# Four graph layers at the edges' nodes: destinations ended in the last aggregation, messages for the source side alone, a head projection of its own

## The reference

```python
# layer 2: attention with 8 heads, self loops included
h = (x @ W_src).reshape(n, 8, 16)
e = leaky_relu(a_src[src] + a_dst[dst])
alpha = softmax of e over the edges of one dst
out = segment_sum(h[src] * alpha, dst) + bias
# layer 3: here `dst` of the layer is the edge's source
h = features @ W_neigh.T + b_neigh
new_h = concat([h[src], abs(h[dst] - h[src])]) @ W_edge.T + b_edge
seg_sum = segment_sum(new_h, dst); cnt = segment_sum(1, dst)
s = (h + seg_sum) / max(cnt, 1)
z = concat([features, s]) @ W_lin.T + b_lin
```

## Time and profile before

| | us |
|---|---|
| median of 3 runs (3661.37 to 3671.05) | 3662.82 |
| profiled execution | 3684.87 |
| its span, first to last instruction | 3683.2 |
| POOL busy | 2036.5 |
| PE busy | 2249.8 |
| DVE busy | 2173.2 |
| ACT busy | 1669.2 |
| mean granted TensorE clock | 0.794 |

### The profile page before, as it was taken

How to read it: one execution, slowest core, us unless ns; L and a number is a source line. 1 busy time by engine, 2 the same in 40 slices (tenths; PEclk the granted TensorE clock), 3 DMA queues, 4 the chain that set the end, 5 groups by cost and what they waited for, 6 DMA issues and landing times. The chain is left out here.

```text
span 3683.2 us, 52863 instructions
## 1 busy us (share of the span) xinstructions
PE 2249.8 (61%) x12839; PEld 1786.9 (49%) x12839; DVE 2173.2 (59%) x7930; ACT 1669.2 (45%) x3697; POOL 2036.5 (55%) x2221
## 2 busy tenths in 40 slices
PE   2316899998999675446556655874553644545442
PEld 1303666766677564446445553553543533333332
DVE  5516998998999686433534636944558533443242
ACT  0016999999998485222322335832441122222100
POOL 3878765665573431468038336703550058888767
PEclk9998999999999877567757757985666667777665
DMA  2511132332331262754266284425330534343363
GB/s 80 170 41 30 44 98 85 101 99 86 99 98 41 81 181 75 195 131 122 60 183 175 60 229 109 116 82 145 93 79 15 160 90 98 85 99 84 58 184 93
DMA packets 592914, 382.51 MB, mean 104 GB/s; under 512 B 50669, under 2 KB 540622, under 8 KB 592266
## 3 DMA queue, kind: packets, MB, share of 16 engines
q1 hardware_dynamic: 537050, 338.44, 31.5%
q0 software_dynamic: 52800, 39.73, 6.1%
q10 hardware_dynamic: 2800, 1.28, 0.3%
HBM read 250.72 MB, written 153.32 MB: 110 GB/s over the span
## 5 line engine op out<-in xcount | busy, mean ns | idle before, releaser
L1290 POOL DMA_INDIRECT p_a<-t_d,k_map_ix x300 | 312.0, 1040 | 431.8 <-DMA p_a<-t_d 378.0
L830 POOL TENSOR_TENSOR a_rs<-a_ve,w_neg_half 128x16 f32<-128x16 f32 x113 | 330.4, 2924 | 241.7 <-DVE a_ve L766 210.5
L856 ACT ACTIVATE a_nr<-a_xb,a_nm,a_rs 128x128 f32<-128x128 f32 x882 | 371.8, 490 | 26.0 <-POOL a_nm L832 26.0
L1787 PE MATMUL c_pq<-layer_src,c_sel 128*128 (+1 forms) x1000 | 243.1, 421 | 163.4 <-ACT c_sel L1757 107.5
L918 PE MATMUL a_ps<-w_ident,a_nr 128*128 128x128 f32 x1568 | 246.4, 281 | 127.5 <-ACT a_ht L864 47.6
L926 PE MATMUL a_ps<-a_ht,w_aug 128*128 128x512 f32 x588 | 315.0, 621 | 2.3 <-DVE a_ht L733 2.3
L918 PEld LDWEIGHTS a_ps<-w_ident,a_nr 128*128 128x128 f32 x1568 | 180.8, 143 | 276.2 <-issue 243.9
L1787 PEld LDWEIGHTS c_pq<-layer_src,c_sel 128*128 128x128 f32 x1000 | 211.4, 299 | 195.4 <-issue 114.0
L1412 PE MATMUL p_pm<-w_aug,p_ht 128*128 128x130 f32 (+1 forms) x1600 | 290.3, 354 | 8.0 <-issue 3.9
L1412 PEld LDWEIGHTS p_pm<-w_aug,p_ht 128*128 128x128 f32 x1600 | 274.4, 260 | 21.3 <-ACT p_ht L1373 11.2
L733 DVE TENSOR_TENSOR a_ht<-a_ps,a_ht 128x512 f32<-128x512 f32 x294 | 203.0, 694 | 136.2 <-ACT a_ps L871 113.3
(11 more groups left out here) (351 smaller groups left out, 6176.1 us busy)
## 6 DMA issues: line engine op xcount, KB each, us to landing
c_a<-t_d SPq DMA_DIRECT2D x125, 256.0 KB
t_d<-c_a SPq DMA_DIRECT2D x125, 256.0 KB
t_s<-p_a SPq DMA_DIRECT2D x100, 256.0 KB
a_xa<-in_x SPq DMA_DIRECT2D x98, 256.0 KB
out<-a_xb SPq DMA_DIRECT2D x98, 256.0 KB, 2.1
p_a<-t_s SPq DMA_DIRECT2D x75, 256.0 KB
p_a<-t_d SPq DMA_DIRECT2D x75, 256.0 KB
t_acc<-q_zt SPq DMA_DIRECT2D x3, 2171.5 KB
```

What stands on the lines that cost most here:

```text
L830: nc.gpsimd.tensor_tensor(RS[:, z, :], VE[:, z, :], w["neg_half"][:, None, 0:J].to_broadcast([P, LNS, J]), ALU.pow).then_inc(s_rstd.sem, 1)
L856: last = nc.scalar.activation(NR[k][:, T.at(NORM[k], 2), cols(j)], normed_rows(T, k)[:, cols(j)], ACT.Identity, bias=NM[:, T.at(1, SHORT), ...
L1290: eng.indirect_dma_start(out=A[:, g, SRC, j, :], out_offset=None, in_=t[f"d{r}"], in_offset=bass.IndirectOffsetOnAxis(ap=k["map_ix"][:, b ...
L1787: last = nc.tensor.matmul(PS[g][:, j, :], SEL[:, g, j, :], keep["src"][:, bass.ds(number(b) * J + j, 1), 0:C].rearrange("p o c -> p (o c)" ...
```

## The change

- `Norms` goes. `Moments.turn` spreads its twelve steps over four tiles as well as over eight.
- `project` loses its kind "normed"; a function of its own, `project_heads`, takes its place. The bias becomes a matmul ahead of each product, the kept rows are copied out by ACT, PE's product stands in the same round as its transposes, and the residual add comes three blocks behind instead of four.
- `aggregate` for layer 2 becomes `finish_destinations`. Behind the addition that gives the destination state it also does layer 3 for the destination side: statistics, normalising, transposes, neighbour features (stored in a new table `gd`), the last product with its bias, and the plain scatter into `out` from POOL, each with a memset behind it.
- `edge_messages` handles the source side alone and loads `gd`. Its loops are written out; POOL alternates gather(n) with scatter(n-4), and each scatter with addition has a memset behind it. Inverse deviations are found on DVE.

```diff
+def project_heads(nc, w, k, t, r, keep):
...
+            LAG = 3
+            for n in range(BLOCKS + LAG):
+                if n <= BLOCKS:
+                    if n < BLOCKS:
+                        there(eng, n)
+                    mo.turn(eng, lambda m: A[:, n % RING, m // J, m % J, :], n, BLOCKS - 1)
+                if 0 <= n - LAG:
+                    residual(n - LAG)
...
+            for n in range(BLOCKS + 1):
+                if n < BLOCKS:
+                    apply(n)
+                if n:
+                    hold(n - 1)
+                if n < BLOCKS:
+                    copy(n)
...
+                    for j in range(J):
+                        nc.tensor.matmul(PM[side][:, j, 0:CW], w["ident"][:, :], BR[:, :], start=True, stop=False)
+                        last = nc.tensor.matmul(PM[side][:, j, 0:CW], HT[:, b % SHORT, side, cols(j)], w["aug2"][:, :], start=False, stop=True)
...
+            for n in range(BLOCKS):
+                turn(n)
+                product(n)
...
+def finish_destinations(nc, w, k, t, r, keep, wm, ws, out):
...
+            for b in range(BLOCKS):
+                eng.wait_ge(s_od, b + 1)
+                for j in range(J):
+                    m = b * J + j
+                    eng.indirect_dma_start(out=out, out_offset=bass.IndirectOffsetOnAxis(ap=k["out_d_ix"][:, m:m + 1], axis=0),
+                                           in_=OD[:, b % 4, j, :], in_offset=None,
+                                           bounds_check=N - 1, oob_is_err=False).then_inc(s_out[b % 4], 16)
+                    if m:
+                        eng.wait_ge(s_idle, m)
+                    nc.gpsimd.memset(IDLE[:, :], 0.0).then_inc(s_idle, 1)
...
+            OUT = 4
+            for n in range(BLOCKS + OUT):
+                if n < BLOCKS:
+                    update(n)
+                if n >= OUT:
+                    output(n - OUT)
+                if n < BLOCKS:
+                    add(n)
+                    eng.wait_ge(s_next, n + 1)
+                if n <= BLOCKS:
+                    mo.turn(eng, lambda m: A[:, n % RING, m, :], n, BLOCKS - 1)
...
+            for n in range(2, BLOCKS + 4):
+                if n < BLOCKS:
+                    widen(n)
+                if 0 <= n - 4:
+                    features(n - 4)
+                if 0 <= n - 2 < BLOCKS:
+                    apply(n - 2)
+                    copy(n - 2)
...
+            for n in range(BLOCKS + 3):
+                if n < BLOCKS:
+                    tiles(n)
+                if 0 <= n - 2 < BLOCKS:
+                    turn(n - 2)
+                if 0 <= n - 3:
+                    product(n - 3)
...
-def edge_messages(nc, w, k, t, r, out):
+def edge_messages(nc, w, k, t, r):
...
+    RING, NORMS, LAG = 7, 4, 4
...
-            stream(eng, *transfers(0), (lambda b, g: nb.invert(eng, b, g), 1), *transfers(1), *transfers(2), *transfers(3))
...
+            def scatter(b, j):
+                m = b * J + j
+                eng.wait_ge(s_tot, b * 2 + j // 2 + 1)
+                if m:
+                    eng.wait_ge(s_acc, 16 * m)
+                eng.indirect_dma_start(out=t["acc"], out_offset=bass.IndirectOffsetOnAxis(ap=k["acc_ix"][:, m:m + 1], axis=0),
+                                       in_=TOT[:, b % NORMS, j, :], in_offset=None, compute_op=ALU.add).then_inc(s_acc, 16)
+                if m:
+                    eng.wait_ge(s_idle, m)
+                nc.gpsimd.memset(IDLE[:, :], 0.0).then_inc(s_idle, 1)
+
+            for n in range(BLOCKS + LAG):
+                for j in range(J):
+                    if n < BLOCKS:
+                        gather(n, j)
+                    if n >= LAG:
+                        scatter(n - LAG, j)
...
-            stream(eng, (stats, 2), (apply, 2), (index, 0), (select, 2), (combine, 2), (messages, 2))
...
+            for n in range(BLOCKS + 3):
+                if n < BLOCKS:
+                    there(eng, n)
+                if n <= BLOCKS:
+                    mo.turn(eng, lambda m: A[:, n % RING, m, :], n, BLOCKS - 1)
+                if 0 <= n - 2 < BLOCKS:
+                    combine(n - 2)
+                if n < BLOCKS:
+                    select(n)
+                if 0 <= n - 3:
+                    messages(n - 3)
...
-            stream(eng, (apply, 0), (copy, 0), (features, 0), (absolute, 0), (totals, 0))
...
+            for n in range(BLOCKS + 2):
+                if n < BLOCKS:
+                    apply(n)
+                    copy(n)
+                    features(n)
+                if 0 <= n - 1 < BLOCKS:
+                    absolute(n - 1)
+                if 0 <= n - 2:
+                    totals(n - 2)
...
-            stream(eng, (turn, 0), (product, 0), (edges, 0))
...
+            for n in range(BLOCKS + 2):
+                if n < BLOCKS:
+                    turn(n)
+                    product(n)
+                if 0 <= n - 1 < BLOCKS:
+                    messages(n - 1)
+                if 0 <= n - 2:
+                    totals(n - 2)
```

More of the change, by code:

```diff
@@ L1083 @@
 SRC, DST = 0, 1
[L1086 to L1137, removed]
@@ L1214, in project @@
     CW = C + 2 * heads
-    first, normed = kind == "first", kind == "normed"
-    sigmoid, norm, overlay = not normed, kind != "plain", not first
+    first = kind == "first"
+    norm, overlay = first, not first
     RING, SHORT = 7, 3
@@ new lines, in edge_messages, with there @@
+        s_load, s_gd, s_sz_out = ([sem(f"{n}{g}") for g in range(RING)] for n in ("load", "gd", "sz_out"))
+        s_kb, s_gt_out = ([sem(f"{n}{g}") for g in range(NORMS)] for n in ("kb", "gt_out"))
+        s_over = [sem(f"over{j}") for j in range(J)]
+        block = ctx.enter_context(nc.Block())
+        cols = lambda j: slice(j * C, (j + 1) * C)
+        uses = lambda b: b // RING + 1
+        def there(eng, b):
+            for j in range(J):
+                eng.wait_ge(s_over[j], 16 * (b + 1))
@@ L2033, in _ @@
+            for g in range(RING):
+                eng.wait_ge(s_sz_out[g], 16 * len(range(g, BLOCKS, RING)))
+            for g in range(NORMS):
+                eng.wait_ge(s_gt_out[g], 16 * len(range(g, BLOCKS, NORMS)))
         @block.gpsimd
         def _(eng):
-            def gather(b, g, what, side, j, s):
-                eng.indirect_dma_start(out=A[:, g, side, j, :], out_offset=None, in_=t[f"d{r}"],
-                                       in_offset=bass.IndirectOffsetOnAxis(ap=IX[:, g, what, j:j + 1], axis=0),
-                                       bounds_check=EP - 1, oob_is_err=False).then_inc(s, 16)
@@ new lines, in messages @@
+            def messages(b):
+                m = b % NORMS
+                eng.wait_ge(s_nh, b + 1)
+                if b >= NORMS:
+                    eng.wait_ge(s_po, (b - NORMS + 1) * 2)
+                v.tensor_tensor(MS[:, m, :, 0:C], PM[:, :, :], w["be_row"][:, None, :].to_broadcast([P, J, C]), ALU.add).then_inc(s_ms, 1)
+            for n in range(BLOCKS + 3):
+                if n < BLOCKS:
[8 more added lines that the diff above has]
+                    messages(n - 3)
@@ new lines, in product @@
+            def product(b):
+                m = b % NORMS
+                eng.wait_ge(s_ht, b + 1)
+                if b:
+                    eng.wait_ge(s_gt, b)
+                nc.tensor.matmul(PG[:, :, :].rearrange("p j c -> p (j c)"), w["wnT"][:, :], HT[:, m, :], start=True, stop=True).then_inc(s_pg, 1)
+                if b:
+                    eng.wait_ge(s_z, b)
+                for j in range(J):
+                    nc.tensor.matmul(PZ[:, j, :], w["ident"][:, :], w["bl_row"][:, :], start=True, stop=False)
+                    last = nc.tensor.matmul(PZ[:, j, :], HT[:, m, cols(j)], w["wlT"][:, 0, :], start=False, stop=True)
+                last.then_inc(s_pz, 1)
@@ L2191, in edges, with messages @@
+            def messages(b):
+                m = b % NORMS
+                eng.wait_ge(s_abs, b + 1)
+                if b:
+                    eng.wait_ge(s_ms, b)
+                for j in range(J):
+                    nc.tensor.matmul(PM[:, j, :], GD[:, b % RING, cols(j)], w["weT"][:, 0, :], start=True, stop=False)
+                    last = nc.tensor.matmul(PM[:, j, :], AD[:, m, cols(j)], w["weT"][:, 1, :], start=False, stop=True)
                 last.then_inc(s_nh, 1)
-                wait(eng, s_ms, b + 1)
```

593 lines of the change are left out of this document (419 added, 174 removed).

## The result

The changed kernel takes 3844.1 us (median of four executions, 3842.7 to 3844.9), against 3662.1 of the kernel before beside it: 1.0495 times as long, 95% interval 1.0472 to 1.0517, or 182 us more. The forecast was 3920 us with a range of 3790 to 4010. The direction and the range hold, and the likeliest value is 76 us too high.

What follows compares the result with a forecast made beforehand. POOL's queue was taken to bound the messages before the change; head projection -34, aggregation +128 and messages +163 gave +257 us on 3684.9, so 3942, or 3920 by the median. The range was 3790 to 4010.

Steps and rivals of the forecast that it cites:

- POOL's queue bounds the messages before: Messages before the change: POOL's own queue, without waits, sets 20.4 us per block, 510 us over 25 blocks.
- two waits: Messages: scatters wait for the former landing, 4.1 us per tile, and each block's tile 0 for totals, 13 us or so.
- The ring: Messages: scatter of tile 0 to the next block's, through last gather and all engines, 29.0 us for 21 blocks; stage 726.
- the gather's landing: Messages: ring term for the last gather from start to seen by DVE, 4.65 us, taken from the projection's trace.
- Start of the messages: Messages: the first scatter comes 45.6 us into the stage, after gathers, DVE's turn and three rounds of ACT.
- The head projection: Head projection: residual add one block earlier makes the chain span three blocks, 7.2 us per block, 34 us less.
- PE's price: Head projection: PE's products, transposes and hand-overs with ACT take 6.8 us per block at full clock, up to 9.5.
- the 8.6 us of before: Head projection before the change: 24 blocks advance in 207 us, 8.6 us each.
- The aggregation: Aggregation with ended destinations: a chain of DVE, ACT and PE over two blocks gives 6.8 us per block, 128 us more.
- the landing rival: Messages: landing of each scatter decides, 4.1 us per tile, stage 461 us, kernel 3655; chance 0.03.
- POOL's queue deciding everywhere: Rival: messages at 13.8 us per block, aggregation at 6.0, 88 us less, kernel 3575; chance 0.08.
- PE at its lower level: Rival: PE stays at its lower clock between long waits, +404 us, kernel 4067; chance 0.09.

Runs made afterwards that it cites:

- e4: Changed kernel with the projection's residual add four blocks behind again instead of three: 3913.2 us, 1.0656 times before.
- e10: Changed kernel without the memset behind each plain scatter of the destinations in the aggregation, the kernel of e7 run again: 3833.6 us.
- e5: Kernel of e1 with the messages' comparison keys loaded only for the first four blocks and reused, on the second chip: 3680.3 us.
- e8: Changed kernel without the four bias matmuls per block in the messages, on the second chip: 3869.3 us.
- e1: Changed kernel with the messages' results five blocks behind the gathers instead of four: 3682.8 us, 1.003 times before.
- e6: Kernel of e1 with sums of even and odd tiles in two tables, added in the edge outputs, on the second chip: 3578.2 us, 0.9764 times before.
- e12: Kernel of e6 run again beside the changed kernel on one chip: 3548.2 us, against 3848.6 of the changed kernel.
- e2: Changed kernel without the memset behind each scatter with addition in the messages: 3850.1 us, 1.0499 times before.
- e7: Changed kernel without the memset behind each plain scatter of the destinations in the aggregation, on the second chip: 3878.4 us.

## Why the prediction was right, and where its sizes were off

*POOL's queue bounds the messages before, and two waits come out from under it.* Right, and both waits were named: the eviction of the totals ahead of the scatter of tile 0 (11 to 12 us in the block shown; the prediction wrote 13 or so), and the landing ahead of the others. DVE waits 20 us per block for the gather, as written. POOL is busy 11.8 us per block (295 over 25), as written.

*The ring, 29.0 us.* Its terms against the block shown: two scatter intervals 8.2 and 8.24; the third scatter with its clear 2.1 and 2.08; the gather from start to seen 4.65 and 2.60; from there to the next scatter 14.1 and 14.43. The term that failed is the gather's landing. The 4.65 came from the projection, where the gather lands while SP loads and stores whole blocks; in e4 the same gather took 4.9 us (2669.04 to 2673.94), with a store and two loads issued between 2668.30 and 2669.25. In the messages the last gather of a block lands in quiet, since SP's burst comes after it, behind DVE's additions. 21 blocks times 1.7 us (2.05 less and 0.3 more) are 36 us, and the stage came out 35 shorter than 726. The nearest row by operation was taken from a stretch with other traffic; that the traffic makes the difference is read from these rows and was not tested for gathers.

The Trainium skill, page DMA: Bandwidth & Descriptors, section Anatomy of one DMA — SWDGE (gpsimd) path, whose fit gave 2.15 us, was the nearer of the two; with it the forecast would have been 3868, 24 us above the result. The 2.60 in the messages agrees with it to half a us. The 4.9 in e4 does not.

*Start of the messages.* The first scatter (3023.68) came 44.1 us behind the first load of the stage, 45.6 into the stage by the prediction.

*The head projection, 7.2 us per block.* That the same ring then spans three blocks was right: e4 shows that the lag is all of the gain. The pace was 6.1 (statistics from 2530.6 to 2678.5, less 2 for the last block's own, over 24). The term that was mis-sized is PE's price. PE was not the last to arrive; the clock was 0.89 over the stage. A round of PE, from the transposes of one block to those of the next, took 5.4 us with a gap of 0.35 for the hand-over where it ran without other waits, and not 6.8 with 1.1:

```profile
2608.21 1.04 PE L1502 MATMUL p_pt<-w_ident,p_ht 128*128 128x128 f32 x8
...
2613.63 1.04 PE L1502 MATMUL p_pt<-w_ident,p_ht 128*128 128x128 f32 x8
```

POOL ran nearly without idle time (its 99 intervals add up to 152.2 us, where 99 times 1.49 are 147.5):

```profile
2663.37 1.00 POOL L1431 DMA_INDIRECT p_a<-t_d,k_map_ix  x1 [0.16 <-issue]
2664.37 0.33 POOL L1436 MEMSET p_idle<- 128x256 f32 x1
2664.86 1.00 POOL L1431 DMA_INDIRECT p_a<-t_d,k_map_ix  x1 [0.16 <-issue]
```

Four gathers with a clear are 6.0 us, the number that the prediction had and set aside. A second slip lies in the 8.6 us of before, which are a mean of two paces. The first six of its 24 intervals took 5.8 us each, since their blocks lie in the ring of seven from the start, and the other 18 took 9.6, about half of the 19.8 read from two blocks. In the changed kernel they took 5.6 and 6.2. So the gain is 18 times 3.4 us, and not 24 times one difference. Over three blocks the old ring is 6.4 us, so close above POOL's 6.0 that it may have a share in the 6.2; no run tells the two apart.

*The aggregation, 6.8 us per block.* The chain of DVE, ACT and PE over two blocks that gave 6.8 was priced too high: the final adds run from 2801.2 to 2933.6, 5.5 us each, and the granted clock in the stretch was 0.85 with the closing part in it. (The terms written down for it add up to 11.75 us, not 12.1.) POOL's plain scatters are the last to end:

```profile
2824.29 0.98 POOL L2163 DMA_INDIRECT out<-c_rows,k_out_d_ix  x1 [0.17 <-issue]
2825.27 0.33 POOL L2168 MEMSET c_idle<- 128x256 f32 x1
2825.76 0.98 POOL L2163 DMA_INDIRECT out<-c_rows,k_out_d_ix  x1 [0.16 <-issue]
```

1.47 us each from 2821.3 to 2968.8 for 100 of them, with 20.1 us ahead of the first and 10.8 to close; e10 confirms it, since taking 0.18 us from each took 15 from the stretch. The prediction had written that this queue would not run without idle time; that was wrong, and is the point at which the term failed. It was a near thing: on the second chip the final adds came 6.2 to 6.4 us apart (e5 to e8), and there the chain decided, as the prediction had it. The reason for adding it, that no other stage runs beside it, was right.

*The rivals.* (The time of the landing rival should read 466 and not 461 for the messages; it changes nothing.) POOL's queue deciding everywhere (3575) and the landing deciding (3655) were rejected because the dependence stands in the code, and rightly. Both came up once the ring was cut: e1 (3683) is bound by the landing, its own term of 4.1 us plus the burst's 3.0 in one of four, and e6 and e12 (3578 and 3548) by the queue at 3.45 per tile. So they were not other accounts of this kernel but the next two floors under its ring. *PE at its lower level* (4067) came in part only: each burst starts there, with the wide product at 2.07 us as the prediction's ring had it, and then the pairs go from 0.63 to 0.39; over the messages the granted clock is 0.62, where it was 0.69.

## What to carry to other kernels

Where an engine's hand-written order alternates the first and the last step of a pipeline, count how many of its own rounds lie between them, and through how many engines: if the last step of a block needs data that the first step issued in the round just before, the whole path is exposed in each block, and one more block of lag was worth more here than any work removed (161 us for one number, against 6 for four matmuls per block and 15 for 100 clears). Take a duration from a row with the same traffic around it, not only the same operation. And when a ring is cut, price the floors under it at once: landing, then collision with bulk loads, then the queue, and look for the one edit that takes out two (two tables in turn: 300 us below the changed kernel, 3.2% below the one before).

## What the runs showed of the hardware that was not expected

- A scatter with addition of 128 rows of 516 bytes and the next one into the same table, which waits for it, start 4.1 us apart in quiet; with 1 MB of bulk traffic issued just behind it, 7.1 in the median of 17 (e1), at most 8.4 (3184.10 to 3192.49); with 0.75 MB, 5.7 (e5).
- A gather is seen 2.6 us after it starts in quiet, and 4.9 us in the traffic of the projection (e4).
- Behind an indirect DMA on POOL the next one starts after 0.30 us. A memset between them ends 0.33 us behind the first, and the next DMA starts 0.17 us behind the memset, so a clear costs 0.18 us where POOL bounds (e10), and nothing where it waits (e2).
- Matmuls taken from the start of a burst shifted those behind them into the stretch at the lower clock level, and the burst got shorter by a third of what was taken out, on the mean of 21 blocks (e8 against e7).
